# A three-layer graph network: update products of four node tiles at once, with the weights held still and the degree scalings kept as rows

## The reference

```python
msg  = concat([h[src], h[dst]]) @ Mw.T + Mb
s1, s2 = segment_sum(msg), segment_sum(msg * msg)       # by dst
mx, mn = segment_max(msg), segment_min(msg)
mean = s1 / degc
var  = relu(s2 / degc - mean * mean)
std  = sqrt(var + STD_EPS)
agg  = concat([mx, mn, std, var])                       # N x 512
h_neigh = concat([agg, agg * (logd / DELTA), agg * (DELTA / logd)])
u = concat([h, h_neigh]) @ Uw.T + Ub                    # N x 1664 by 1664 x 128
u = batch_norm(u * sqrt(1 / N))
out = leaky_relu(u @ mix_w.T + mix_b, 0.01) + h
```

## Time and profile before

| | us |
|---|---|
| median of 3 runs (2147.47 to 2161.76) | 2148.81 |
| span of the profiled execution | 2141.7 |
| POOL busy | 1235.7 |
| DVE busy | 1096.6 |
| PE busy | 682.6 |
| ACT busy | 455.6 |

### The profile page before, as it was taken

One profiled execution on the slowest core, in us unless ns is written; L12 is line 12 of the kernel. 1 busy time (PEld: TensorE's weight loads), 2 busy tenths in 40 slices (PEclk: granted clock), 3 DMA queues, 4 the chain that ended last, 5 costly groups with the idle time before them and its releaser, 6 DMA issues. The chain is left out here.

```text
span 2141.7 us, 10446 instructions
## 1 busy us (share of the span) xinstructions
PE 682.6 (32%) x2156; PEld 402.8 (19%) x2156; DVE 1096.6 (51%) x2178; ACT 455.6 (21%) x1024; POOL 1235.7 (58%) x1358
## 2 busy tenths in 40 slices
PE   5611233132322470323132232362113322233265
PEld 5311121011111230112111111131101211112122
DVE  8600755464644843445464463572525664466464
ACT  0103321122111154111111111136101221112125
POOL 7673666676666127745675675406756666576504
PEclk9975666565655685566565666686556666656677
DMA  4363333333333033323332232204323333333200
GB/s 59 105 167 113 93 103 103 91 99 92 92 91 91 18 112 113 111 66 99 96 101 76 88 103 75 65 27 145 106 84 101 93 88 93 88 103 96 76 0 30
DMA packets 97107, 190.18 MB, mean 89 GB/s; under 512 B 30792, under 2 KB 56984, under 8 KB 97040
## 3 DMA queue, kind: packets, MB, share of 16 engines
q0 software_dynamic: 59968, 160.78, 26.6%
q1 hardware_dynamic: 37077, 28.77, 4.9%
HBM read 168.75 MB, written 17.75 MB: 87 GB/s over the span
## 5 line engine op out<-in xcount | busy, mean ns | idle before, releaser
L742 POOL DMA_INDIRECT G<-p_by_rank,index x774 | 734.8, 949 | 560.2 <-issue 227.8
L742 POOL DMA_INDIRECT G<-p_by_node,index x387 | 367.4, 949 | 225.0 <-issue 120.3
L921 PE MATMUL ps<-wide_ident,agg 128*128 128x128 f32 x288 | 80.3, 434 | 1209.3 <-issue 701.2
L1470 DVE TENSOR_TENSOR ps<-ps,G 128x1024 f32<-128x1024 f32 (+3 forms) x222 | 250.3, 1127 | 191.2 <-issue 78.4
L921 PEld LDWEIGHTS ps<-wide_ident,agg 128*128 128x128 f32 x288 | 51.5, 217 | 1239.5 <-issue 721.9
L936 PE MATMUL ps<-w_u_sb,aggT 128*128 128x384 f32 x576 | 284.3, 654 | 0.0
L1714 DVE SCALAR_TENSOR_TENSOR var<-tot,rdeg,msq 128x128 f32<-128x128 f32 x75 | 26.1, 348 | 426.4 <-ACT msq L1109 407.8
L936 PEld LDWEIGHTS ps<-w_u_sb,aggT 128*128 128x128 f32 x576 | 162.6, 282 | 144.7 <-issue 119.1
L1135 ACT ACTIVATE u_sb<-ps 128x128 f32<-128x128 f32 x75 | 20.7, 277 | 721.1 <-remote 509.0
L1472 DVE TENSOR_TENSOR ps<-ps,G 128x512 f32<-128x512 f32 (+3 forms) x222 | 141.6, 638 | 0.0
L1471 DVE TENSOR_TENSOR ps<-ps,G 128x512 f32<-128x512 f32 (+3 forms) x222 | 141.5, 637 | 0.0
(11 more groups left out here) (280 smaller groups left out, 1328.3 us busy)
## 6 DMA issues: line engine op xcount, KB each, us to landing
G<-p_by_rank,index POOLq DMA_INDIRECT x774
p_by_rank<-base SPq DMA_DIRECT2D x18, 512.0 KB
G<-p_by_node,index POOLq DMA_INDIRECT x387
p_by_node<-G SPq DMA_DIRECT2D x6, 514.0 KB
w_u_sb<-in_w_u SPq DMA_DIRECT2D x3, 768.0 KB
x_r<-rows_by_rank SPq DMA_DIRECT2D x1, 1600.0 KB
G<-shared_rows SPq DMA_DIRECT2D x12, 53.0 KB
windows<-src_pad SPq DMA_DIRECT2D x1, 624.8 KB, 14.1
```

Of the source, the lines that this page charges most:

```text
L742: g.indirect_dma_start(G[:, n % R, j, 0:w], None, table, bass.IndirectOffsetOnAxis(ap=named, axis=0))\
L921: ins = nc.tensor.transpose(ps[:, 2, i * D:(i + 1) * D], agg[:, t % 2, i * D:(i + 1) * D], ident[:, :])
L1470: TT(run[:, 0:nk, :], run[:, 0:nk, :], G[:, n % R, 0:nk, 0:2 * D], ALU.add)
```

## The change

The products of stage A are made for four tiles at once, and the other way round. The batches are tiles 0 to 3, 4 to 7, up to 20 to 23; the last tile stays alone and is done as before.

- `update(l, b, k)` holds a 128x128 block of weights still and streams 512 columns, the `hT` and the turned aggregates of four tiles. For each of the three products k that is five matmuls, ten records, and its result is already turned. One k is issued behind the `turn` of each of three tiles in the next batch; for the last batch all three follow `turn(23)`.
- The per-tile copies of the product, `turn_update` and the copy of the update are gone for tiles 0 to 23. `combine(l, b)` on DVE makes 512 columns in four instructions, two tiles after the last product was issued. Since the node is now the column, `amp` and `att` are needed as rows: they are transposed once in the first layer, stored to DRAM and read back to all partitions (`scale_row`, 3.3 MB).
- `agg` has four buffers in place of two; the turned aggregates of all tiles are kept in `base`. The ACT stream has the copy of `turn(t-1)` behind the root of tile t.
- ACT begins 16 of the tiles from three gathered slots and the own row as the fourth column, in six instructions in place of three, and DVE's `own_rows` goes for these. The number of slots and gathers stays.
- PE's `lend` (sums of the last tile's lent columns) comes after `turn(0)` and not after tile 1. The accumulators of the last tile lie in SBUF. The input rows for the output are loaded a second time in the last layer.

```diff
+    BATCH = 4
+    PB = [(t, min(BATCH, T - 1 - t)) for t in range(0, T - 1, BATCH)]
+    AR = 4
+    DUE = {(b + 2) * BATCH: b for b in range(NB - 2)}
+    Z_BANK = (5, 4, 7)
+    ORDER = (1, 2, 0)
...
-            def update(l, t):
-                z = ps[:, 4, 0:3 * D]
...
-                if t >= 1:
-                    pe.wait_ge(u_ready.sem, u_ready.at(l, t))
-                mm(z, hT[:, hot(t)], w_own[:, :], start=True, stop=False)
-                pe.wait_ge(agg_copied.sem, agg_copied.at(l, t + 1))
+            def update(l, b, k):
+                t0, nt = PB[b]
+                z = ps[:, Z_BANK[k], 0:nt * D]
+                of = slice(k * D, (k + 1) * D)
+                if k == ORDER[0]:
+                    if b == 0:
+                        pe.wait_ge(w_ready.sem, w_ready.at(l, 1))
+                        pe.wait_ge(borrowed.sem, borrowed.at(l, 1))
+                    else:
+                        pe.wait_ge(u_ready.sem, u_ready.at(l, b))
+                    pe.wait_ge(base_ready.sem, base_ready.at(l, NC - chunk_of[t0 + nt - 1]))
+                    pe.wait_ge(agg_copied.sem, agg_copied.at(l, t0 + nt))
+                mm(z, w_own[:, of], hT[:, t0 * P:(t0 + nt) * P], start=True, stop=False)
+                zt = z.rearrange("p (t d) -> p t d", d=D)
                 for i in range(4):
-                    ins = mm(z, aggT[:, t % 2, i * D:(i + 1) * D], w_u_sb[:, i, :], start=False, stop=i == 3)
+                    ins = mm(zt, w_u_sb[:, i, of], aggT[:, t0:t0 + nt, i, :], start=False, stop=i == 3)
                 ins.then_inc(z_done.sem, 1)
...
-                    if t <= FAR:
+                    if t < T - 1:
                         turn(l, t)
-                        if t >= 1:
-                            update(l, t - 1)
-                        if t >= 2:
-                            turn_update(l, t - 2)
...
+                        b, i = divmod(t - BATCH, BATCH)
+                        if b >= 0 and i < 3:
+                            update(l, b, ORDER[i])
+                        if t == T - 2:
+                            for k in ORDER:
+                                update(l, NB - 1, k)
...
-                    if n + 1 in END and END[n + 1] <= FAR:
-                        if END[n + 1] >= 2:
-                            copy_product(l, END[n + 1] - 2)
-                        if END[n + 1] >= 3:
-                            copy_update(l, END[n + 1] - 3)
...
+                    if n - 1 in END and 1 <= END[n - 1] < T - 1:
+                        copy_turned(l, END[n - 1] - 1)
+                    if n - 2 in END and END[n - 2] == T - 2:
+                        copy_turned(l, T - 2)
...
-            def combine(l, t):
-                U, z = u_sb[:, t % 2, :], ps[:, 4, :]
-                dve.wait_ge(z_copied.sem, z_copied.at(l, t + 1))
+            def combine(l, b):
+                t0, nt = PB[b]
+                z0, z1, z2 = (ps[:, bank, 0:nt * D].rearrange("p (t d) -> p t d", d=D) for bank in Z_BANK)
+                amps, atts = (scale_row[:, k, t0 * P:(t0 + nt) * P].rearrange("p (t d) -> p t d", d=D) for k in range(2))
+                U = uT[:, t0:t0 + nt, :]
...
+                dve.wait_ge(z_done.sem, z_done.at(l, 3 * b + 3))
+                ch.step(TT(U, z1, amps, ALU.mult))
+                ch.step(TT(z2, z2, atts, ALU.mult))
+                ch.wait()
+                ch.step(TT(U, U, z0, ALU.add))
+                ch.wait()
+                STT(U, z2, v_sb[:, 5:6], U, ALU.add, ALU.add).then_inc(u_ready.sem, 1)
...
+                    if n in END and END[n] in DUE:
+                        combine(l, DUE[END[n]])
...
+                    if n == tile_groups[T - 1][0]:
+                        combine(l, NB - 2)
...
+                    if n == tile_groups[T - 1][-3]:
+                        combine(l, NB - 1)
```

More of the change, by code:

```diff
@@ L152, in build @@
         GROUPS.append((AT[a % 2 * 4], -2, a // 2, 4))
+    BESIDE = []
     for t in range(T):
@@ L157, in build @@
         sizes = [GW] + [rest] * (rest > 0) + [GW] * (full - 1)
+        if rest and 0 < t < T - 1:
+            BESIDE.append(t)
+            full, rest = divmod(PLAN_T[t] - k0 - (GW - 1), GW)
+            sizes = [GW - 1] + [rest] * (rest > 0) + [GW] * full
         if t == T - 1:
@@ L491, in hot, with tiles @@
             return slice(t * P, (t + 1) * P)
+        def tiles(c):
+            t0, nt = CH[c]
+            return slice(t0, t0 + nt)
         def cols(c):
@@ L571, in shared_rows @@
                 for n, (t, _, _, _) in enumerate(GROUPS):
+                    if l == L - 1 and n == tile_groups[t][0] and t - 1 in DUE:
+                        b = DUE[t - 1]
+                        load_input(*PB[b], 3 * b + 3)
                     if not shared_slots[n]:
@@ L607, in _ @@
             shared_rows(L - 1)
+            for b in range(NB - 2, NB):
+                load_input(*PB[b], 3 * b + 3)
+            load_input(T - 1, 1, NZ)
         @block.gpsimd
@@ L985, in mix @@
                     pe.wait_ge(biased.sem, biased.at(l, c))
-                mm(ps[:, 0, 0:w], w_mix_bn[:, :], uT[:, cols(c)], start=True, stop=True).then_inc(mixed.sem, 1)
+                mm(ps[:, 0, 0:w].rearrange("p (t d) -> p t d", d=D), w_mix_bn[:, :], uT[:, tiles(c), :], start=True, stop=True).then_inc(mixed.sem, 1)
             def variances(l, c):
@@ L1100, in begin @@
                     act.wait_ge(low_ready.sem, low_ready.at(l, t))
-                f(run, G[:, n % R, :, 0:2 * D], ACT.Copy)
-                f(top, G[:, n % R, :, 0:D], ACT.Copy)
-                f(low, G[:, n % R, :, 0:D], ACT.Copy).then_inc(begun.sem, 1)
+                k = GROUPS[n][3]
+                f(run[:, 0:k, :], G[:, n % R, 0:k, 0:2 * D], ACT.Copy)
+                f(top[:, 0:k, :], G[:, n % R, 0:k, 0:D], ACT.Copy)
+                last = f(low[:, 0:k, :], G[:, n % R, 0:k, 0:D], ACT.Copy)
+                if t in BESIDE:
+                    act.wait_ge(extras_done.sem, extras_done.at(l, 1))
+                    act.wait_ge(base_ready.sem, base_ready.at(l, NC - chunk_of[t]))
+                    if t in AT:
+                        act.wait_ge(dve_used.sem, dve_used.at(l, len(AHEAD)))
+                    f(run[:, k, :], base[:, t, S1:S2 + 1, :].rearrange("p a d -> p (a d)"), ACT.Copy)
+                    f(top[:, k, :], base[:, t, TOP, :], ACT.Copy)
+                    last = f(low[:, k, :], base[:, t, LOW, :], ACT.Copy)
+                last.then_inc(begun.sem, 1)
             def square_mean(l, t):
@@ L1472, in accumulate @@
                 TT(low[:, 0:nk, :], low[:, 0:nk, :], here, ALU.min).then_inc(dve_used.sem, 2 if j == 1 else 1)
-                if j == 1:
+                if j == 1 and t not in BESIDE:
                     own_rows(l, n)
@@ L1587, in take_singly @@
                     low_of = TT(into[2], least, row[:, 0:D], ALU.min)
-                    sums, most, least = into
                     if i < nk - 1:
@@ L1615, in borrow @@
                     rows = base[:, T - 1, own, :]
-                    ch.step(TT(rows, rows, ps[:, 5, i * D:(i + 1) * D], op))
+                    last = TT(rows, rows, ps[:, 5, i * D:(i + 1) * D], op)
+                    ch.step(last) if i == 2 else last.then_inc(borrowed.sem, 1)
                 ch.wait()
+                dve.wait_ge(borrowed.sem, borrowed.at(l, 1))
             def own_weights(l):
```

231 lines of the change are left out of this document (117 added, 114 removed).

## The result

The changed kernel takes 2088.47 us (median of 4 runs, 2086.57 to 2093.21) against 2148.14 for the kernel before: ratio 0.971, interval 0.967 to 0.975. It is faster, by 60 us where 141 were forecast.

A forecast was written before the change was run, and what follows sets the result against it. The prediction took POOL's gathers, paused by PE's late completions, as the bound. From 2141.7 us span and 7 around it, -175 + 45 - 15 + 4 = -141 gave 2008 us; own range 1975 to 2045, wide range 1935 to 2115.

The forecast's parts named there:

- What bounds: POOL's gathers pause because the ring is full, as PE's completions arrive late while gathers run; 243.1 us of waits could go.
- the 32.7 us at the start: One POOL wait for ACT before the first tiles get going, ACT being busy with the first projection; expected to stay.
- 2.5 us a record, whatever the width: Price of each PE matmul record while POOL gathers, about two gathers; the number on which the forecast rests.
- Fewer records, -175 us: PE's records beside the gathers fall from 340 to 238 a layer, so 68 of 243.1 us of POOL's pauses stay.
- With the same rate now: 595 - 2.57 p = 496 + p: Second layer's balance: each us of pause p clears 2.57 us of PE's lateness, 496 us being the gathers; p = 28 us.
- DVE's work, -15: Some 0.9 us a tile less on DVE, free beside gathers; shorter lag behind the last gather gains 5 us a layer.
- The tail, +45: End of stage A: combine, last batch's 30 records, combine, last product and idle products run serially, +15 us a layer.
- The rows of scalings, +4: The 3.3 MB broadcast, two transposes and one copy, mostly hidden by the wait for the first combine; between 0 and +12.
- rival 2: Short pauses clear less lateness, so POOL's waits fall only by a third, 81 us: 2098 us; chance 0.12.
- Rival 1: PE's lateness is absorbed wholly and POOL waits only for the 32.7 us at the start: 1936 us; chance 0.12.
- Rivals 3 and 4: Slower: lateness not by records, 2183 us, chance 0.11; or late state never cleared, 2329 or about 2250, chance 0.06.
- rival 3: Lateness goes by POOL's stream, not records; POOL waits as before and the tail is paid: 2183 us, slower; chance 0.11.

The follow-up runs named there:

- e4: Changed kernel with five more 16-column float32 products ahead of each part of a batch, 150 records a layer more beside the gathers: 2159.23 us, late.
- e18: Changed kernel without the products of the maxima and minima, two of four aggregates (output not the reference's): 2087.99 us, late (kernel before 2148.74).
- e17: Changed kernel with VectorE again adding the own rows of all tiles, 48 VectorE instructions a layer more: 2116.76 us, late.
- e9: The changed kernel itself, run again in time: 1792.98 us against 1751.69 for the kernel before, ratio 1.024.
- e10: Changed kernel with another order at the end of stage A (own PSUM bank, combines moved, no idle products): 1754.98 us, in time, ratio 1.0016 to kernel before.

## Why the prediction was right in direction and wrong in size

- **What bounds.** Right: POOL waits because the ring is full, and completions come late while it gathers. That the pauses hang on lateness is borne out in time, where the changed kernel has none of them; the 32.7 us at the start, which the prediction took as fixed, are gone there too.
- **2.5 us a record, whatever the width.** Right, a little low: 2.7 over records of 16, 128 and 512 columns (e4).
- **Fewer records, -175 us. This is the step that failed.** It measured -78. "With the same rate now: 595 - 2.57 p = 496 + p" treats TensorE as the only engine that is late, and the pauses as its balance. Neither holds. The low price is not the reason: with 2.75 us a record the same balance leaves 36 us of pauses in the second layer in place of 28, and 56 were measured (552.5 - 496). e18 took 56 records a layer more away, ScalarE no longer waited for TensorE's turns, and the pauses stayed at 167 us; so these are no longer set by TensorE's records. What the traces show in its place is VectorE waiting for its own completions, 115.1 us at L1761 where it was 13.6; that this alone keeps the pauses is not shown, and what holds the later stages at 550 to 553 us is open. And e4 added 150 records a layer for 24 us of time, so the cleared lateness doesn't go by the pauses' length.
- **DVE's work, -15.** The path was right and the size too small. The own rows are worth 28 us (e17), 20 of them where the prediction looked, in VectorE's lag behind the last gather: in the second stage the last tile's first group ended 28.6 us behind it before (1406.62 against 1378.04) and 20.2 now. That the work is free beside the gathers holds for the second and third stage, and not for the first (7 us). What it missed is that VectorE, once it no longer waits for ScalarE, waits for itself.
- **The tail, +45.** Right: +41 in time, its pieces as worked out, 38 of them removed by order (e9, e10). Late, the ends of the stages lengthened by 24 us, against 45 - 15 = 30, and the second stage's transposes came 48.5 us behind the last gather, where 57 less the smaller lag was forecast.
- **The rows of scalings, +4.** No run tests it apart; in time the changed kernel with the new tail is within 4 us of the kernel before.
- **The rivals.** The measured time lies in the wide range (1935 to 2115) and outside the forecast's own (1975 to 2045), next to rival 2's 2098. That is not support for rival 2: its mechanism, short pauses that clear less, was not tested by itself. Rival 1 (all absorbed) failed, 171 us of pauses are left. Rivals 3 and 4 forecast a slower kernel; late it is faster, and its pauses fell. In time the kernel is slower by the tail, which is half of rival 3's sum, but not by its mechanism. Rival 3 leaned on the Trainium skill ("SBUF — State Buffer", Who interferes with whom), that PE and ACT wait on nobody. There the page speaks of engines that contend for SBUF's ports. A completion that is seen late is another matter, so neither the 23.59 us of before nor any late trace here speaks for or against the rule, and the rule was no ground for rival 3.
- **Not foreseen at all**: that the bound I worked from belongs to a condition outside the kernel, and that the sign of the result turns with it. By the tail's own term, which I had right, a reader could have asked what the change is worth if nothing is late: 2 to 3% slower.

## What to carry to other kernels

When one engine's lateness seems to fill a ring, taking its work away may show nothing, because another wait stands where it stood. Look at whose waits grow when the time stands still, and cut both engines' work in one experiment under the condition that is in question. Split the span into the stretch of the gathers and the ends of the stages before crediting a change to either. Batching instructions trades their number for a burst at the end, and the burst stood in the traces of both conditions: give the last batch its own order (a bank of its own, the combine behind the last tile) before judging the batching. And where a gain rests on a stall that no instruction explains, time the old kernel in several sets of runs first.

## What the runs showed of the hardware

In the late traces, while POOL issued indirect DMAs at 1.25 us each, matmul records came through at one per 2.7 us on average, 16 to 512 columns wide, and a turn was seen up to 63 us after its records had ended (e4: the records end at 980.7, the copy starts at 1043.43, 19.8 us into a pause of POOL). VectorE saw its own last instruction 2.7 us late, 30 times in the changed kernel. The same traces lack the gathers' landings (2181 of 18576 semaphore updates, against 18571 in time). Whole sets of runs had this and others, with the same kernel before, had none of it: 2149 against 1751 us. The cause is not shown.
